# A three-layer graph network on one core: layer 0's indirect gathers issued in pairs behind TensorE's semaphores, not in runs of 18

## The reference, cut to what matters

```
def conv(h, W, b):
    m = concatenate([h[dst], h[src], edge_attr], axis=1) @ W + b
    return segment_sum(m, dst, num_segments=n_nodes)
h = relu(conv(x, W1, b1)); h = relu(conv(h, W2, b2))
out = layernorm(x + conv(h, W3, b3))
```

## Time and profile before

| | |
|---|---|
| median of three runs | 3386.24 us |
| span of the profiled execution, first to last instruction | 3233.6 us |
| runs' median less that span | 152.6 us |
| TensorE, VectorE, ScalarE, GpSimd busy | 83%, 59%, 62%, 49% |
| mean granted TensorE clock | 0.92 of full speed |

### The profile page before, as it was taken

How to read it: one execution, slowest core, us unless ns; L and a number is a source line. 1 busy time by engine, 2 the same in 40 slices (tenths; PEclk the granted TensorE clock), 3 DMA queues, 4 the chain that set the end, 5 groups by cost and what they waited for, 6 DMA issues and landing times.

```text
span 3233.6 us, 53485 instructions
## 1 busy us (share of the span) xinstructions
PE 2694.7 (83%) x19203; PEld 1774.2 (55%) x19203; DVE 1908.8 (59%) x4349; ACT 2019.4 (62%) x2852; POOL 1593.4 (49%) x1391
## 2 busy tenths in 40 slices
PE   2588898998898898898876888889898688888887
PEld 0145454454454455454444565656566577777776
DVE  7778887887887787787742222222233255555554
ACT  5577787786787777777702444444444367777776
POOL 5414234234234224324235565566562767777774
PEclk9689999999999999999987898889899699999999
DMA  4523343433333343343354666666666467777774
GB/s 93 141 85 101 126 134 101 153 105 100 131 125 101 118 140 99 120 139 101 133 194 137 195 207 196 200 197 224 197 222 204 150 211 237 232 236 240 233 237 131
DMA packets 257349, 519.43 MB, mean 161 GB/s; under 512 B 153953, under 2 KB 189783, under 8 KB 253888
## 3 DMA queue, kind: packets, MB, share of 16 engines
q1 hardware_dynamic: 152596, 299.50, 28.2%
q10 hardware_dynamic: 57404, 146.14, 12.0%
q0 software_dynamic: 47088, 70.34, 9.3%
HBM read 361.98 MB, written 153.81 MB: 160 GB/s over the span
## 4 chain that ended last, share of the span: by engine, by line
PE 68%; another core or an unknown queue 10%; DVE 8%; ACT 7%; issue 6%; POOL 1%; DMA 1%; ACTq 1%; SPq 0%; DVEq 0%; POOLq 0%
PE ps L1591 18%; PE ps L1576 15%; PE ps L1547 12%; PE ps L1605 9%; ACT spread L996 6%; PE ps L1637 3%; PE ps L1624 2%; PE ps L1676 2%; DVE is_key L1219 2%; PE ps L1677 2%; PE ps L1641 2%; ACT blocks L931 1%; DVE is_low L1209 1%; PE ps L1662 1%
## 5 line engine op out<-in xcount | busy, mean ns | idle before, releaser
L869 POOL DMA_INDIRECT far_rows<-parts,far_src x1350 | 1541.3, 1142 | 1571.4 <-DMA far_src<-in_src 852.4
L931 ACT ACTIVATE blocks<-ps 128x505 fp8e4<-128x505 f32 x1875 | 1128.9, 759 | 369.3 <-PE ps L1547 264.2
L996 ACT CAST spread<-blocks 125x1500 fp32r<-125x1500 fp8e4 x517 | 734.5, 1442 | 540.7 <-PE ps L1591 415.5
L1576 PE MATMUL ps<-blocks,parts 125*128 125x375 fp8e4 x3560 | 969.3, 335 | 17.6 <-issue 13.2
L1460 DVE CAST spread<-blocks 125x1500 fp32r<-125x1500 fp8e4 x468 | 447.8, 961 | 813.5 <-PE ps L1591 652.9
L1547 PE MATMUL ps<-is_key,is_low 128*128 128x505 bf16 x1875 | 718.1, 393 | 192.1 <-DVE is_key L1219 103.1
L1219 DVE TENSOR_SCALAR is_key<-from_one,parts 128x500 bf16<-128x500 f16 x1875 | 591.3, 346 | 70.0 <-PE ps L1547 50.5
L1591 PE MATMUL ps<-spread,halves_last 125*128 125x376 f32 x2500 | 517.1, 353 | 122.7 <-ACT spread L996 68.9
L1591 PEld LDWEIGHTS ps<-spread,halves_last 125*128 125x128 f32 x2500 | 430.2, 194 | 183.3 <-ACT spread L996 105.0
L1576 PEld LDWEIGHTS ps<-blocks,parts 125*128 125x128 bf16 x3560 | 326.3, 101 | 274.1 <-issue 76.5
L1547 PEld LDWEIGHTS ps<-is_key,is_low 128*128 128x128 bf16 x1875 | 186.2, 100 | 440.0 <-DVE is_key L1219 163.7
(11 more groups left out here) (146 smaller groups left out, 1591.3 us busy)
## 6 DMA issues: line engine op xcount, KB each, us to landing
blocks<-counts SPq DMA_DIRECT2D x250, 937.5 KB
counts<-blocks ACTq DMA_DIRECT2D x25, 4687.5 KB, 14.6
far_rows<-parts,far_src POOLq DMA_INDIRECT x1350
far_masks<-far_masks_kept SPq DMA_DIRECT2D x50, 281.2 KB
attr_stage<-in_edge_attr SPq DMA_DIRECT2D x125, 88.0 KB
far_masks_kept<-far_masks SPq DMA_DIRECT2D x25, 281.2 KB, 11.9
h_rows<-rows ACTq DMA_DIRECT2D x49, 128.0 KB
own_sb<-attr_sums ACTq DMA_DIRECT2D x49, 95.7 KB
```

Source lines behind the costliest of these rows:

```text
L869: nc.gpsimd.indirect_dma_start(far_rows[:, g % 2, j, :], None, parts_d[layer], bass.IndirectOffsetOnAxis(ap=far_src[:, g % BATCHES, j:j + ...
L931: nc.scalar.activation(blocks[:, b % 2, :, n * W:(n + 1) * W], build[:, c % BUILD, 0:COLS].rearrange("p (t w) -> p t w", w=W), ACT.Copy, s ...
L996: nc.scalar.copy(spread[0:L, u % SPREAD_RING, :, 0:DENSE], counted(g, t, T)).then_inc(act_spread, 1)
L1576: nc.tensor.matmul(acc_ps(g), parts[0:L, layer % 2, whole_tile(layer, t), 0:2, :].rearrange("p k d -> p (k d)"), moving, start=alone, stop ...
```

## The change

The run of gathers in layer 0 is cut up. GpSimd's loop now runs over 24 passes and ten points in each. Point 0 lies at the start of a pass, and point p (1 to 9) behind unit p-1. At each point GpSimd waits for a semaphore that TensorE raises there, and then issues two gathers (one at point 9). These are 19 per pass, while a batch has 18, so the batch that is being fetched moves ahead of the pass bit by bit. The order of the gathers is the same, and so are the waits of a batch's first gather. Where none of TensorE's existing semaphores marks the end of a unit (units 0, 2, 5 and 7), the last matmul of `apply_narrow` raises a new one, `narrowed`. In passes 1 and on, `deg_turned` and `turned` stand in for it behind units 0 and 2.

```diff
+    NARROW_ENDS = [0, 2, 5, 7]
+    RELEASES = UNITS
...
-            for g in range(BATCHES):
-                for j in range(FJ):
-                    gather_rows(g, j)
+            def wait_release(g, point):
+                if point == 0:
+                    if g:
+                        pool.wait_ge(far_summed, g)
+                    return
+                u = point - 1
+                if u in SUM_AFTER:
+                    pool.wait_ge(attr_summed, g * PER_BATCH + SUM_AFTER.index(u) + 1)
+                elif g and u == 0:
+                    pool.wait_ge(deg_turned, g)
+                elif g and u == 2:
+                    pool.wait_ge(turned, g)
+                else:
+                    pool.wait_ge(narrowed, g * len(NARROW_ENDS) + NARROW_ENDS.index(u) + 1)
+            gathered = 0
+            for g in range(BATCHES - 1):
+                for point in range(RELEASES):
+                    wait_release(g, point)
+                    for n in range(gathered, min(gathered + (2 if point < RELEASES - 1 else 1), BATCHES * FJ)):
+                        gather_rows(*divmod(n, FJ))
+                        gathered = n + 1
...
                         if u == UNITS - 1:
                             last.then_inc(applied, 1)
+                        elif u in NARROW_ENDS:
+                            last.then_inc(narrowed, 1)
```

More of the change, by code:

```diff
@@ L348, in gnn_kernel @@
         far_summed = sem("far_summed")
+        narrowed = sem("narrowed")
         attr_kept = sem("attr_kept")
@@ L875, in gather_batch @@
                     gather_rows(g, j)
-            for g in range(BATCHES):
-                for j in range(FJ):
-                    gather_rows(g, j)
+            def wait_release(g, point):
[19 more added lines that the diff above has]
+                        gathered = n + 1
+            assert gathered == BATCHES * FJ
             for g in range(BATCHES, ALL):
```

## The result

| | before | after |
|---|---|---|
| median of the runs | 3386.54 us (3382.51 to 3394.11, 4 runs) | 3197.41 us (3190.29 to 3211.03, 4 runs) |
| ratio, 95% interval | | 0.9436 [0.9406, 0.9466] |
| profiled execution: run time, span | not known, 3233.6 us | 3190.29 us, 3188.5 us |

A forecast was written before the change was run, and what follows sets the result against it. Long gather runs were taken to delay TensorE's semaphores in layer 0. Savings of 35 (pass 0), 110 (passes 1 to 13) and 15 us (14 to 17) total 160: 3386.2 - 160 = 3226 us, own range 3195 to 3255, 8-in-10 range 3170 to 3290.

The forecast's parts named there:

- What bounded the kernel: Layer 0: TensorE's semaphores seem to reach other engines late during a long run of gathers, stalling everything; a few cost nothing.
- A clean pass: Layer 0 pass without the stall: 51.2 us against a mean 60.5; after giving back 0.8 for VectorE, 8.5 us saved.
- Pass 0: Layer 0, 140 to 181 us: splitting the run of 36 gathers removes 35 us; first copy starts near 226.
- Which passes get short runs: Layer 0 queue model: only pairs by conv up to pass 13, saving 110 us; from 14 the run continues at conv.
- Passes 14 to 17: Layer 0: run at conv as long as before but ending earlier; if the stall ends with it, 15 us saved.
- Passes 18 to 23: Layer 0: 18 gathers back to back from the same time as before, nothing saved; passes of 58 to 62 us.
- From the span to the time: Whole kernel: 160 us off the 3233.6 us span gives 3073; the runs' median, 152.6 us above that span, gives 3226.
- The semaphore waits for the gather in progress: Rival, layer 0: a pair at point 8 still stalls about 2.5 us; clean passes gain 5.2, total 3271 us; chance 0.16.
- Every pass is clean: Rival, layer 0: a queue fed by pairs never stalls TensorE, so 244 us go, giving 3142 us; chance 0.08.
- The gathers cost the same wherever they are: Rival, layer 0: the same 450 gathers cost 9.3 us per pass, only spread out; 3386 us; no-gain chance 0.05.
- Each pair holds VectorE: Rival, layer 0: the slow second gather recurs in each of 9.5 pairs, 73 us per pass, 3510 us; chance 0.06.
- 8 to 10 long waits, 50 to 65 us in total: Sign in the profile after: VectorE's copy of conv keeps this many long waits, in place of 23.

The follow-up runs named there:

- run_early: Kernel before, but all 18 gathers of batch b go out in one run at point 0 of pass b: 3393.25 us, ratio 1.0496.
- even_pairs: Kernel before with layer 0's gathers in pairs at fixed points, 18 per pass (batch 0 in fours): 2973.99 us, ratio 0.919.
- mixed: Against before: layer 0 grouped by batch (18s, half-row 18s, nines, sixes, twelve and six, pairs), layer 1 partly spread over units: 3085.82 us, ratio 0.9525.
- again: The kernel before, unchanged, profiled a second time: 3263.62 us, span 3261.8; the 13 runs beside it have a median of 3236.87 us.
- layer1_units: even_pairs plus layer 1's 18 gathers spread behind the pass's units, against before on unaffected chips: 2757.21 us, ratio 1.0001; repeats 0.9998 and 0.9999.
- after_2: The change itself, run once more against the kernel before on an unaffected chip: 2758.17 us, ratio 1.0001.

## Why the prediction was right, and where it was wrong

**What bounded the kernel.** Right where the kernel is affected: in layer 0 the stall comes beside the run of gathers, it goes with the run when that is moved (run_early), and it is gone when the run is cut into pairs (even_pairs). The traces also fit the mechanism that I gave, TensorE's semaphores that reach the others late while gathers go out. That is an inference from who waits; no view shows a semaphore on its way. In run_early the builds' semaphore is late and in pass 21 of after `attr_summed` is, so it isn't one semaphore, and it isn't the traffic of the gathers, since halving their rows does nothing. Why they come late on one chip and not on the next, and in layers 0 and 1 but hardly in layer 2, is open. No run here gives the cause.

**A clean pass.** 51.2 us was worked out from single units, and 51.1 to 51.2 was measured. The 0.8 us that I gave back for VectorE at 96% wasn't needed: TensorE never waits for it. That is 13 x 0.8 = 10 us, and 7 of them show in passes 1 to 13 (117.1 for 110).

**Pass 0.** 37.4 for 35, and the first copy at 222.3 for 226.

**Which passes get short runs.** The model of the queue was nearly right. Passes 1 to 11 are clean, 12 and 13 lose 2 us each (53.2 and 52.9), and from 14 on runs stall. Since mixed shows that six gathers in a row cost 2 us, a queue that is empty by `conv` has already cost something, and the boundary is soft.

**Passes 14 to 17.** 15 us predicted, 7.8 found. The step that failed is "If the stall ends with the run, that saves" 15 us, with "as many gathers as before" at `conv`. The stall begins at whichever wait on TensorE comes first in a long enough run, as in the timeline of pass 21: in unit 7, where 11.88 to 14.07 us go by in passes 15 to 17, and not at `conv` in unit 8.

**Passes 18 to 23.** 0 predicted, 18.5 us lost. The two traces are probably of different chips, and the kernel before has passes of 61.5 us (again) and 60.5 in its two traces, so I can't say how much of these 3 us per pass is the chip and how much is the change. On the unaffected chip the same passes take 51.1.

**From the span to the time.** "152.6 us above that span" was read as something that every run has around it. It is 1.8 us (3190.29 less 3188.5). Added on both sides, the error drops out of the difference. What it hid doesn't: the saving was read from a trace in which before is 150 us faster, and applied to runs that are slower. The runs give 189 us in place of 160, which are the 29 us by which 3226 was too high. Where these 29 us lie is an estimate, since no trace of before at 3387 us exists. With the layers 1 and 2 of the trace after (1686.3 us), its layer 0 would end at 3384.7 - 1686.3 = 1698 us, against 1646 in the trace of before and 1669 in again. Its passes 1 to 23 would be 62 to 63 us long, and the change would save 11 us in a clean pass and not 9. That 3197 still lies in the range is luck in part: 3 us more of saving would have put it outside.

**The rivals.** *The semaphore waits for the gather in progress*: out, since pairs at point 8 leave the pass at 51.1. *Every pass is clean*: out for this change, but it is what even_pairs gives once the drift is taken away, and it was worth 263 us where I had priced it at 244. *The gathers cost the same wherever they are*, with the Trainium skill's rule behind it (SBUF — State Buffer, "Who interferes with whom": "PE and ACT never wait on anyone"): even_pairs and run_early, with the same gathers at 2974 and 3393 us on one chip, rule it out as a forecast. Read as a rule about ports it isn't contradicted, for on the unaffected chip TensorE is busy 27.00 of 27 us beside a run. On the affected ones TensorE does wait, but, as far as the traces tell, for engines that wait for its semaphores. *Each pair holds VectorE*: out, VectorE is busy 49.71 us in a pass of 51.1 with nine and a half pairs.

**What was to be seen.** Pairs 4.9 us apart, the full stretch from 140 to 181, the first copy and the lengths of the early passes came as said. "8 to 10 long waits, 50 to 65 us in total" at the copy did not: there are 2, of 8.1 us together, since the stall is now met by other lines first, as by line 1251 in pass 21. Looking only at the copy one would have thought it gone. Passes 18 to 23 take 61.7 to 65.4 us where 58 to 62 was said. No `sum_far` of layer 0 waits for gathers.

**The best version.** On affected chips even_pairs should beat the change: it takes 0.919 [0.9141, 0.9239] of before on one of them, and the change 0.9436 on another. The two were not timed on one such chip, but even_pairs has clean late passes and the change hasn't. layer1_units adds the cut in layer 1, which mixed measured at 4.6 us per pass, or some 100 us over 22 passes (an estimate). The whole of it was timed on unaffected chips alone, where it equals before (0.9998 and 0.9999).

## What to carry to other kernels

When all engines stop together for several microseconds, and the profile names no reason, look at what the one engine that is still busy does, and move that: where the stall goes with it, it takes part in the cause, though it needn't be all of it (layer 2 has the same runs and hardly a stall). Spread descriptor work that needs not be in a run over the points at which its data can be there, and keep the count per cycle equal to the need, or the schedule drifts into the old run. And compare a profiled execution's span with its own run time before its microseconds are added to another run's median; where only the median of other runs is known, a large difference may be another chip, on which the loss to be saved has another size.

## What the runs showed of the hardware

- The same kernel takes 2757, 3237 and 3241 us on three chips, and 3387 in the first comparison, whose chip isn't known: up to a factor of 1.23. 13 runs on one of the chips lie within 1.4% (3211.39 to 3255.74). With pairs in layer 0 (fours in its pass 0) the difference nearly goes from that layer: it ends at 1398.8 (even_pairs, affected) and 1395.4 us (after_2, unaffected).
- On an affected chip, in layers 0 and 1, a run of indirect gathers seems to delay what waits for TensorE. In layer 0 a run of two costs nothing, one of six between nothing and 4.1 us, one of 18 some 10.7 us, with 128 rows or with 64. In layer 2 of the same chips runs of 18 cost about 0.6 us per pass.
- A stall is paid twice: in pass 9 of run_early the granted clock was 1.00 ahead of the stall, 0.84 in it and 0.90 over the 44.7 us behind it.
